# A Mamba-2 and ternary FFN layer pair on one core: the slot's order of work rearranged on all engines

## The reference

```python
x = x + mamba(layernorm(x))
x = x + ffn(layernorm(x))

# mamba(h), with H = 32 heads of P = 64 channels, state N = 64, G = 8 groups, K = 4 taps
x = rmsnorm(h, norm_w)
z, xBC, dt_raw = split(x @ in_proj_w)            # 2048, 3072, 32
xBC = silu(causal_depthwise_conv(xBC, conv_w, 4 taps) + conv_b)
xs, B, C = split(xBC)                            # 2048, 512, 512
dt = softplus(dt_raw + dt_bias);  dA = exp(-exp(A_log) * dt)
h_t = dA_t * h_(t-1) + (dt_t * x_t) B_t          # per head, a 64 x 64 state
y_t = h_t C_t + D * x_t
g = y * silu(z);  g = g * rsqrt(mean over the group of g^2 + eps) * gate_norm_w
out = h + g @ out_proj_w

# ffn: layernorm, ternary(w1), gelu, layernorm, ternary(w2)
```

## Time and profile before

| | |
|---|---|
| median of 3 runs | 1142.57 us (1141.39 to 1144.17) |
| the profiled execution's own time | 1145.73 us |
| its span | 1143.9 us |
| PE busy | 1033.2 us (90%), 8912 products |
| DVE busy | 1059.9 us (93%) |
| ACT busy | 970.0 us (85%) |
| POOL busy | 868.6 us (76%) |
| granted clock of PE, whole span | 0.959 |

### The profile page before, as it was taken

One profiled execution on the slowest core, in us unless ns is written; L12 is line 12 of the kernel. 1 busy time (PEld: TensorE's weight loads), 2 busy tenths in 40 slices (PEclk: granted clock), 3 DMA queues, 4 the chain that ended last, 5 costly groups with the idle time before them and its releaser, 6 DMA issues.

```text
span 1143.9 us, 26227 instructions
## 1 busy us (share of the span) xinstructions
PE 1033.2 (90%) x8912; PEld 732.0 (64%) x8912; DVE 1059.9 (93%) x2004; ACT 970.0 (85%) x2836; POOL 868.6 (76%) x596
## 2 busy tenths in 40 slices
PE   1724789999999999999999999999999999996797
PEld 1603566676666666676666666766666666664576
DVE  7597999999999999999999999999999999989474
ACT  2767898999999999999999999999999999984464
POOL 7300356888888888888888888888888888885765
PEclk9955899999999999999999999999999999997899
DMA  6320000000000000000000000000000000021001
GB/s 170 117 86 0 10 1 2 1 1 2 1 30 2 2 2 29 2 2 2 29 2 2 2 29 2 2 2 29 2 1 1 21 1 2 1 78 46 1 29 46
DMA packets 28084, 22.58 MB, mean 20 GB/s; under 512 B 11696, under 2 KB 22576, under 8 KB 27824
## 3 DMA queue, kind: packets, MB, share of 16 engines
q1 hardware_dynamic: 25136, 20.90, 5.9%
q10 hardware_dynamic: 2816, 0.02, 0.1%
HBM read 12.78 MB, written 8.13 MB: 18 GB/s over the span
## 4 chain that ended last, share of the span: by engine, by line
PE 77%; DVE 14%; issue 3%; POOL 2%; ACT 2%; DMA 0%; POOLq 0%; DVEq 0%; ACTq 0%
PE bank L1713 10%; PE bank L1695 10%; PE bank L1625 8%; PE bank L1727 8%; PE bank L1641 8%; PE bank L1626 6%; PE bank L1627 6%; PE bank L1681 5%; PE bank L1662 5%; DVE conv L1191 4%; PE bank L1766 3%; PE bank L1738 2%; DVE lm L1181 2%; PE bank L1555 1%; PE bank L1746 1%
## 5 line engine op out<-in xcount | busy, mean ns | idle before, releaser
L1191 DVE SCALAR_TENSOR_TENSOR conv<-bank,cw,conv 128x509 f32<-128x509 f32 (+2 forms) x576 | 421.7, 743 | 16.6 <-ACT conv L762 8.6
L636 POOL TENSOR_TENSOR lm<-lm,cbs 128x1024 f32<-128x1024 f32 x128 | 304.3, 2377 | 75.7 <-ACT xw L866 75.7
L1181 DVE TENSOR_TENSOR_SCAN lm<-bank,ident 128x512 f32<-128x512 f32 x256 | 298.7, 1210 | 0.7 <-PE bank L1641 0.6
L911 ACT ACTIVATE xdt<-bank,dt_all 128x64 f32<-128x64 f32 x1024 | 222.3, 329 | 37.2 <-PE bank L1662 37.2
L866 ACT ACTIVATE xw<-xdt,lm 128x64 f32<-128x64 f32 x768 | 199.3, 365 | 0.0
L644 POOL TENSOR_TENSOR ssum<-ssum,sq 128x512 f32<-128x512 f32 x96 | 123.1, 1283 | 93.0 <-ACT sq L926 92.8
L1625 PE MATMUL bank<-xn_hi,w_hi 128*128 128x512 f32 x320 | 166.1, 519 | 13.8 <-DVE conv L1191 13.1
L615 POOL TENSOR_TENSOR gated<-gated,gate 128x512 f32<-128x512 f32 x128 | 164.9, 1288 | 15.9 <-DVE gated L1238 14.5
L626 POOL TENSOR_TENSOR gated<-gated,rbs 128x512 f32<-128x512 f32 x120 | 153.8, 1282 | 0.0
L877 ACT ACTIVATE conv<-bank,cb_bias,cw 128x512 f32<-128x512 f32 x189 | 142.6, 781 | 11.5 <-PE bank L1627 7.3
L1713 PEld LDWEIGHTS bank<-lm,xdt 128*64 128x64 f32 x2048 | 110.3, 137 | 63.7 <-issue 63.7
(11 more groups left out here) (217 smaller groups left out, 1766.5 us busy)
## 6 DMA issues: line engine op xcount, KB each, us to landing
lm<-in_L_attn_in_proj_w SPq DMA_DIRECT2D x1, 2048.0 KB, 11.7
xn_scratch<-chan SPq DMA_DIRECT2D x4, 512.0 KB, 4.6
r_stage<-residual_scratch SPq DMA_DIRECT2D x8, 256.0 KB, 2.9
xn_stage<-xn_scratch SPq DMA_DIRECT2D x7, 256.0 KB, 3.2
x_scratch<-r_stage SPq DMA_DIRECT2D x7, 256.0 KB, 2.0
gate<-in_L_attn_hidden_states SPq DMA_DIRECT2D x2, 512.0 KB, 4.6
cdec<-in_L_attn_hidden_states SPq DMA_DIRECT2D x2, 512.0 KB, 7.1
w_out<-in_L_attn_out_proj_w SPq DMA_DIRECT2D x8, 128.0 KB, 3.3
```

The source lines that it names most:

```text
L636: gp.tensor_tensor(lm[:, mr, :, :], lm[:, mr, :, :], cbs[:, :, :], ALU.mult).then_inc(m_done, 1)
L911: act.activation(xdt[:, r, at:at + HP], misc_of("xt", n)[:, at:at + HP], ACT.Copy, scale=dt_h).then_inc(xdt_done, 1)
L1181: V.tensor_tensor_scan(lm[:, m % R, a, :], bc_bank[(3 * m + a) % 2][:, :], ident4[:, :], 0.0, ALU.mult, ALU.add).then_inc(scanned, 1)
L1191: V.scalar_tensor_tensor(out=conv[:, ci % 4, shift:S], in0=tile_bank(b, n, t)[:, 0:S - shift], scalar=cw[:, q, t, KW - 1 - shift:KW - shif ...
```

## The change

1. Output: `gated` becomes the stationary operand and `w_out` the moving one, one product per chunk of 128 tokens; `out_bank` then holds tokens on partitions, and `copy_output`, `last_output` and their two semaphores go. DVE adds the residual straight from `out_bank`, in slot 14 and not in slot 15.
2. `pend` holds the chunk ends of all slots and batches. They are made once, in slot 4 of batch 0, by 16 products of `sel` with the chunk-end columns of `pr_parts` into `out_bank` and one DVE copy. `chunk_products` goes.
3. Step 0 of the states moves from DVE to ACT (`first_state`).
4. The root's spread moves from ACT to POOL, and with `root` from r = 0 to r = 1.
5. PE: `states`, `y_within`, `y_states` stand side by side (`inner`), the rows k = 2 and k = 0 before them, k = 1 behind. Tile 3 of r = 1 is projected at the end of r = 0 (`next_tile`), `variance` and `cb_products` come late in r = 0, `gate_tile` last in r = 1.
6. ACT: the weighing for the second slot is done in the first (`weigh(1)` at r = 0), then the C·B copies, the early tile's convolution and the variance copy; `gate_silu` comes last in r = 1.
7. DVE: taps in longer runs, steps 1 and 2 after the product; the next input's low half moves from the end of slot 7 to behind the scans of slot 8. The two heads' scans stay two instructions.
8. The misc banks' plan follows. `qdiag`, `dtb`, `alog`, `aexp` share memory.

```diff
-XO_SLOT = LAG_OUT
+XO_SLOT = LAG_OUT - 1
...
+def early_tile(b, n, t):
+
+    return n % R == 1 and t == PLAN[1][0] and (b, n) != (0, 1)
...
             n = 4 * q + r
+            plan += [(n, "xt", LAG_SSD, 0), (n, "s", LAG_STATE, 0)]
             if r == 0:
-                plan.append((n, "var", LAG_VAR, 0))
-            if r < 2:
-                plan += [(n, "s", LAG_STATE, 0), (n, "xt", LAG_SSD, 0)]
-            else:
-                plan += [(n, "xt", LAG_SSD, 0), (n, "s", LAG_STATE, 0)]
-            if r == 0:
-                plan += [(n, "cb", LAG_SSD, 0), (n, "cb", LAG_SSD, 1)]
+                plan += [(n, "cb", LAG_SSD, 0), (n, "cb", LAG_SSD, 1), (n, "var", LAG_VAR, 0)]
             if r == 1:
-                plan.append((n, "bt", LAG_M, 0))
-                plan.append((n, "rbc", LAG_FACTOR, 0))
+                plan += [(n, "bt", LAG_M, 0), (n, "rbc", LAG_FACTOR, 0)]
             if n == XO_SLOT:
-                plan.append((n, "xo", SLOTS, 0))
+                plan.append((n, "unused", SLOTS, 0))
...
-        pend = sb("pend", [P, 4, CH])
+        pend = sb("pend", [P, SLOTS, NCH])
...
+                    after(gp, rstd_done, UNITS, bb, v)
+                    after(gp, rbc_ready, UNITS, bb, v - 1)
+                    gp.tensor_copy(rexp[:, :, :], rtok[:, :].unsqueeze(2).broadcast_to([P, 2 * CH, HP])).then_inc(rexp_done, 1)
...
                 if r == 0:
                     decay_product()
                     normalise()
+                elif r == 1:
+                    normalise()
                     root()
+                    decay_product()
+                    square_sum()
...
+                def first_state():
...
+                    after(act, s_ready, SLOTS, bb, m)
+                    after(act, y_ready, SLOTS, bb, m - 2)
+                    act.activation(hpk[:, m % 2, 0, :], misc_of("s", n)[:, 0:NS], ACT.Copy).then_inc(hfirst, 1)
+
+                def next_convolve():
+                    if real and early_tile(b, n + 1, PLAN[1][0]):
+                        begin(PLAN[1][0], n + 1)
...
                     weigh()
                     convolve()
                     activate(0)
+                    scale_x()
+                    first_state()
+                    square()
+                    gate_silu()
+                    weigh(1)
+                    copy_cb()
+                    next_convolve()
                     copy_variance()
+                elif r == 1:
+                    convolve()
+                    activate(0)
+                    first_state()
                     scale_x()
                     square()
-                    gate_silu()
-                    copy_cb()
-                elif r == 1:
-                    convolve()
-                    weigh()
-                    activate(0)
-                    if not (b == NB and n == 9):
-                        expand_root(b, n)
-                    scale_x()
-                    square()
-                    gate_silu()
                     copy_bt()
                     copy_factor()
+                    gate_silu()
                 elif r == 2:
                     convolve()
                     weigh()
+                    first_state()
                     scale_x()
                     activate(0)
                     square()
-                    copy_output()
                     activate(1)
                     gate_silu()
...
+                next_low()
                 if r == 0:
-                    taps(0, 1)
-                    state_step(0)
-                    taps(1, 2)
+                    taps(0, 3)
+                    chunk_ends()
                     state_step(1)
-                    taps(2, 3)
                     state_step(2)
+                elif r in (1, 2):
+                    taps(0, 3)
                     chunk_ends()
-                elif r == 1:
-                    taps(0, 1)
-                    state_step(0)
-                    taps(1, 2)
+                    taps(3, 4)
                     state_step(1)
-                    taps(2, 3)
-                    state_step(2)
-                    taps(3, 5)
-                    chunk_ends()
-                    taps(5, 6)
-                elif r == 2:
-                    taps(0, 2)
-                    state_step(0)
-                    taps(2, 3)
-                    state_step(1)
-                    taps(3, 4)
-                    chunk_ends()
                     taps(4, 5)
                     state_step(2)
                     taps(5, 6)
                 else:
-                    state_step(0)
-                    taps(0, 1)
+                    taps(0, 2)
                     chunk_ends()
-                    taps(1, 2)
+                    taps(2, 3)
                     state_step(1)
-                    taps(2, 3)
                     state_step(2)
...
-                    last = MM(out_bank[:, :], w_out[:, m, :], gated[:, (m // R) % 2, m % R, :], start=(m == 0), stop=(m == SLOTS - 1))
+                    for c in range(CH):
+                        tok = slice(P * c, P * c + P)
+                        last = MM(out_bank[:, tok], gated[:, (m // R) % 2, m % R, tok], w_out[:, m, :],
+                                  start=(m == 0 and c == 0), stop=(m == SLOTS - 1 and c == CH - 1))
...
+                def inner():
+
+                    states()
+                    y_within()
+                    y_states()
 
                 if r == 0:
                     out_product()
                     tiles()
-                    variance()
-                    states()
+                    transposes()
                     gate_tile()
-                    transposes()
-                    y_within()
                     rows(ssd, 2)
                     rows(ahead, 0)
-                    y_states()
+                    inner()
+                    rows(ahead, 1)
                     cb_products()
+                    next_tile()
+                    variance()
                 elif r == 1:
                     tiles()
-                    states()
                     transposes()
-                    out_product()
-                    y_within()
                     rows(ssd, 2)
                     rows(ahead, 0)
-                    y_states()
-                    gate_tile()
+                    inner()
+                    rows(ahead, 1)
+                    out_product()
                     b_transposes()
                     factor_transposes()
+                    gate_tile()
                 elif r == 2:
                     tiles()
                     transposes()
-                    states()
+                    rows(ssd, 2)
+                    rows(ahead, 0)
+                    inner()
+                    rows(ahead, 1)
                     out_product()
-                    y_within()
+                    gate_tile()
+                else:
+                    tiles()
+                    transposes()
+                    out_product()
+                    gate_tile()
                     rows(ssd, 2)
...
+                if n == R:
+                    ends = pr_parts[:, :].rearrange("k (c i) -> k c i", i=P)[:, :, P - 1:P].rearrange("k c i -> k (c i)")
+                    for m in range(SLOTS):
+                        last = MM(out_bank[:, NCH * m:NCH * m + NCH], sel[:, m, HP:HP + P], ends, start=True, stop=True)
+                    last.then_inc(pend_ready, 1)
```

More of the change, by code:

```diff
@@ L331, in build @@
         s_ready = sem("s_ready")
+        hfirst = sem("hfirst")
         hstep = sem("hstep")
@@ L872, in convolve, with begin @@
                     for t in PLAN[r]:
-                        ci = CONV_ORDER.index((q, t))
-                        after(act, proj_ready, NCONV, b, ci)
-                        after(act, silu_done, NCONV, b, ci - 4)
-                        act.activation(conv[:, ci % 4, :], tile_bank(b, n, t)[:, :], ACT.Identity,
-                                       scale=cw[:, q, t, KW - 1:KW], bias=cb_bias[:, q, t:t + 1]).then_inc(acc_init, 1)
+                        if not early_tile(b, n, t):
+                            begin(t, n)
+                def begin(t, n):
+                    ci = CONV_ORDER.index((q, t))
+                    after(act, proj_ready, NCONV, b, ci)
+                    after(act, silu_done, NCONV, b, ci - 4)
+                    act.activation(conv[:, ci % 4, :], tile_bank(b, n, t)[:, :], ACT.Identity,
+                                   scale=cw[:, q, t, KW - 1:KW], bias=cb_bias[:, q, t:t + 1]).then_inc(acc_init, 1)
                 def activate(k):
@@ L1569, in misc_free @@
                     who = back(bb, pn, lag) if pkind != "xn" else following(bb)
-                    if who is not None:
+                    if who is not None and pkind != "unused":
                         break
@@ L1582, in misc_free @@
                 elif pkind == "s":
-                    after(pe, hstep, 3 * SLOTS, wb, 3 * wm + 2)
```

(1 more changed line is left out.)

131 lines of the change are left out of this document (50 added, 81 removed).

## The result

The changed kernel takes 1169.63 us (median of 4 runs, 1169.01 to 1170.45), the kernel before 1142.44 beside it: a ratio of 1.0237, 95% interval 1.0219 to 1.0255. It is 2.4% slower. The forecast was 1152, slower, with a range up to 1165; the sign was right and the size was a third of what came. The profiled execution took 1170.01 us with a span of 1168.2; the one of before had a span of 1143.9. The 24.3 us between the spans are what has to be found. (The medians are 27.2 us apart, because the profiled execution of before took 3.3 us more than its median and that of the change 0.4.)

A forecast was written before the change was run, and what follows sets the result against it. TensorE set the pace with VectorE just behind; relieving TensorE alone could win 0.5 of 28.6 us per four slots. Profiled 1145.7 + 9 (loop) + 1.5 (start) - 1 (end) = 1155.2, or 1152 in the median's terms; range 1131 to 1165.

The forecast's parts named there:

- PE's side: TensorE per group of four slots: fewer seams save 1.3 us (0.4 to 1.8), output about 0; it no longer binds.
- DVE's own work: VectorE per group of four slots: eight copies out, -0.80 us; six dependent pairs at 0.135, +0.81; stays 28.0 to 28.1.
- (a): First tap of r = 1: C·B waits for state step 2, then ScalarE's copies and convolution; VectorE waits 0.30 us.
- (b): Second tile of r = 2: its bank is freed late by r = 1's gate on ScalarE; VectorE's tap waits 0.2 us.
- (c): r = 2 to 3, on ScalarE alone: convolution to next convolution takes 8.2 us against VectorE's 8.0; wait 0.2.
- Sum of waits 0.8 per quad: Loop, per group of four slots (quad): VectorE's waits total 0.8 us against 0.5 now, making the group 0.3 longer.
- Rival A: VectorE alone sets the pace; waits vanish, the loop wins 0.3 to 0.5 us per four slots: 1129 to 1136; 30%.
- B: Rival: the loop's waits stay just as large as now, giving 1140 to 1145 us; 12%.
- C: Rival: TensorE's idling lowers its clock in the loop, some 1.5 us per fall, giving 1159 to 1170 us; 8%.
- 0 hidden to 1.8 exposed, 1.5 taken: Start: TensorE's 16 small chunk-end products and VectorE's 512-column copy cost 1.5 us, as both engines stand still.
- At the end the transposes of the output go ... -1 taken: End: output transposes go and a 2.26 us wait moves one FFN step earlier; -3 to +2 us, -1 taken.
- POOL has it by about 13, so it is hidden: GpSimd's root spread, 1.0 us, is ready before TensorE wants it at about 13.8 after the group's start: no cost.

The follow-up runs named there:

- apart_r0: The changed kernel with VectorE's order at r = 0 alone made tap, chunk-end copies (cdec), tap, state step, tap, state step: 1157.5 us.
- gate_first: The changed kernel with the gate's tile of r = 1 ahead of the B and factor transposes on TensorE, its SiLU ahead of their copies on ScalarE: 1161.8 us.
- variance_later: four_together with the variance moved behind the tile of r = 1, the early tile left behind C times B: 1140.2 us.
- tile_first: The changed kernel with the early tile of r = 1 ahead of C times B on TensorE, its start ahead of their copies on ScalarE: 1187.8 us.
- five_together: four_together plus the early tile of r = 1 in front of C times B: 1169.7 us.
- root_drain: The changed kernel with GpSimd's root and spread in the drain put back in front of feed-forward steps 0 and 2: 1162.7 us.
- four_together: The changed kernel with root_drain's, apart_r0's and gate_first's edits and the chunk-end products behind slot 3: 1142.3 us, ratio 0.9984 to the kernel before.

## Why the forecast had the sign and not the size

By its own terms, as the spans show them: loop +9 forecast, +11.9 measured; start +1.5, +4.4; end -1, +8.0. Of the 14.8 us that are missing, 9.0 are the end's, 2.9 the start's and 2.9 the loop's (4.8 without the group of before at a lower clock).

**PE's side** was right in kind. States to y_within is 0.39 or 0.40 in each slot (565.77 to 566.17), the output product's eight pieces are 0.81 to 0.89 as forecast. Per group PE's busy time fell from 28.88 (115.54 of 115.60 times 28.89) to 28.20, by 0.7, where I took 1.3 and bounded it by 0.4 and 1.8. It changed nothing, as forecast. The Trainium skill says that changing the tiling mode drains the engine (TensorEngine Tiling (Array Packing), Key Properties), and the seam of 0.11 agrees; a reader who stopped there would have forecast a gain.

**DVE's own work**: -0.80 and +0.81 were to cancel. Busy time per group went from 28.63 to 28.56. Three dependent taps are 2.20 in a row now (557.70 to 559.90), 3 x 0.65 + 2 x 0.125. Each pair costs 0.125 by these rows and 0.10 to 0.115 by apart_r0: the forecast's 0.135 was somewhat high, and the cancelling is real, if not whole (six pairs at 0.12 are 0.73 of the 0.80). This is the point at which the change gives back what it takes off DVE.

**The waits.** (a) C·B was to start 5.75 after the scans of r = 0 and does at 5.79 (590.36 - 584.57); the first tap of r = 1 was to come at 8.78 and does at 8.74 (564.19 - 555.45), late by 0.27 against 0.30 forecast. (b) The tap forecast at 17.55 comes at 17.87, late by about 0.3 (573.32 - 572.36 less 0.65) against 0.2; gate_first prices it at 0.24. (c) 0.12 against 0.2. The late state copy of r = 3 was to cost 0.1 and costs 0.08 (582.66 to the step at 583.40 is 0.74, less the tap's 0.66). So these waits are as forecast, 0.77 against 0.8.

The step that failed in the loop is "Sum of waits 0.8 per quad": it has no term for the fourth wait, 0.19. I followed variance in PE's queue as work before z's end, in (b), and not as what stands in front of the tile of r = 1. That wait is most of what is missing in the traced group, which was to take 28.9 and takes 29.12; variance_later, without it, has slots of r = 1 shorter by 0.19.

Over all groups the loss is 0.40 per group, 0.46 without the one of before at a lower clock, where 0.3 was forecast. Rival A (no waits) and B are out; C is out for the change, whose granted clock in the loop is 1.00 in all windows, with PE idle for 4% of the time. What C describes came in tile_first and five_together, at 1.6 us for each fall where C had 1.5.

**ACT and POOL.** ACT's state copy takes 0.11 of its queue (553.57 to 553.68), under my 0.2; the estimate of 0.15 from the figures of the Trainium skill (ScalarE: Activation LUTs, What ACT_TABLE_LOAD costs) was nearer, and both were too high. POOL's spread is 0.61 and not 1.0, and hidden in the loop.

**The start.** The step that failed is "0 hidden to 1.8 exposed, 1.5 taken". I priced the products and the copy (1.13 and 0.69, each right) and not their place: the copy waits for all that PE has queued ahead of them, C·B and a tile at half the clock, 4.48. The edit that moves 16 instructions on PE brings the start back to that of before (141.43 and 141.36).

**The end.** The step that failed is "At the end the transposes of the output go ... -1 taken", with "POOL has it by about 13, so it is hidden" in the part on POOL. That was worked out in the loop. I listed the root and the spread as moved from r = 0 to r = 1 and followed them past POOL's products, but not past the feed-forward steps that stand between the same two slots in the drain. My upper bound for the case without that cover, "up to 1", was 7.0 by root_drain, the clock's part in it included. This one omission is 7.0 of the missing 14.8. Whether the -1 for the output's transposes and the result rows was right can't be told: the end that is left, 136.7 against 135.7, is inside the scatter. The sign came from the loop, which was worked out wait by wait; most of the missing size is the end's, which was not.

## What to carry to other kernels

A step moved by one slot in a pipelined loop moves past everything that stands between these slots in the prologue and the drain as well: write down, for each engine, its queue there, and not only in the steady loop. In a queue served in order, the place of a short instruction decides more than its length: 16 products of 1.1 us cost 4.3 behind a tile that ran at half the clock, and nothing where PE was idle anyway, and a tile that seems only late can be the cover for the handover of a bank behind it. List every instruction that waits on another engine and ask what stands in front of what it waits for: the one wait of the loop that I left out was 0.19 of 0.96 us per group. And when copies are taken off a full engine, look at what they stood between: here the dependent neighbours that came together gave back nine tenths of it, and parting them again, with two other reorderings and the root's, was worth the 2.4%.

## What the runs showed of the hardware that I hadn't expected

A broadcast copy of 128x512 on GpSimd takes 0.61 us, half of a two-operand pass over the same elements (1.27), while the power of only 128x8 elements takes 1.65 (L653, L623 and L650 above). And TensorE's granted clock reaches into a wait's price. In the change PE was busy for 5.10 of the 14 us from 1070 to 1084, and in the 6 us behind them the clock was 0.54, so the lower level, 1.2 GHz, for most of it; the four transposes of the factor took 1.11 and not 0.6. With the root earlier PE was busy for 10.0 of the same 14 us, the clock was 0.92 in them and not 0.83, and 0.78 in the 6 us behind. In the change's loop, gaps of 0.2 to 0.3 us that add up to 4% left it at 1.00; in tile_first, with waits of 0.77, it fell in five of 30 groups, for 1.6 us each. And equal orders of work can end 8 us apart: the ends of four_together and five_together, 134.7 at a clock of 0.94 and 142.5 at 0.86.
